# Decoder layer on one core: another PSUM bank for the x1 transposes, the denominators turned by a transpose, and the router's weight halves side by side in one matmul

## The reference

```
x  = layernorm(x + self(x))       # softmax(x x^T / 16), entries under 0.01 taken out, rest times x, plus a term of W
x  = layernorm(x + cross(x, ctx)) # 16 heads of 16: q, k, v with biases, masked softmax, @ Wo + bo
x  = layernorm(x + ffn(x))        # probs = softmax(x @ Wr) over 8 experts, top 2; sum of p_e * (x @ Wi[e]) @ Wo[e]
```

## Time and profile before

| | us |
|---|---|
| median of 3 runs (lowest, highest) | 889.59 (889.4, 890.37) |
| the profiled execution | 888.66 |
| its span, first to last instruction | 886.9 |
| TensorE busy (matmul) / loading weights | 846.5 / 737.9 |
| VectorE busy | 725.9 |
| ScalarE busy | 654.0 |
| GpSimd busy | 199.8 |
| mean granted TensorE clock | 0.993 of full |

### The profile page before, as it was taken

How to read it: one execution, slowest core, us unless ns; L and a number is a source line. 1 busy time by engine, 2 the same in 40 slices (tenths; PEclk the granted TensorE clock), 3 DMA queues, 4 the chain that set the end, 5 groups by cost and what they waited for, 6 DMA issues and landing times.

```text
span 886.9 us, 25688 instructions
## 1 busy us (share of the span) xinstructions
PE 846.5 (95%) x7972; PEld 737.9 (83%) x7972; DVE 725.9 (82%) x2772; ACT 654.0 (74%) x1961; POOL 199.8 (23%) x293
## 2 busy tenths in 40 slices
PE   4789999999999999999999999999999999999985
PEld 3678888888888888888888888888888988888874
DVE  3557888888888888888888888888888888888765
ACT  2468877777887777788777777877777787777760
POOL 2212222221222222222222222222222222222101
PEclk9899999999999999999999999999999999999998
DMA  8544444444334444433344443334444333433300
GB/s 257 159 120 98 106 104 106 105 120 98 93 99 101 103 107 120 99 91 99 98 110 106 117 103 93 99 98 107 105 116 115 85 99 95 107 79 85 85 12 11
DMA packets 89830, 91.09 MB, mean 103 GB/s; under 512 B 19440, under 2 KB 85600, under 8 KB 89696
## 3 DMA queue, kind: packets, MB, share of 16 engines
q1 hardware_dynamic: 89696, 89.45, 40.0%
HBM read 26.84 MB, written 3.67 MB: 34 GB/s over the span
## 4 chain that ended last, share of the span: by engine, by line
PE 89%; DVE 3%; SPq 3%; ACT 2%; issue 2%; DMA 1%; POOL 1%; POOLq 0%; DVEq 0%; ACTq 0%
PE psum L1024 22%; PE psum L908 18%; PE psum L899 10%; PE psum L924 10%; PE psum L974 7%; PE psum L967 7%; PE psum L956 3%; PE psum L988 3%; PE psum L945 1%; PE psum L981 1%; PE psum L938 1%; PE psum L950 1%; ACT x1T L483 1%; DMA wout_sb<-in_wout 1%; DVE mix L608 1%
## 5 line engine op out<-in xcount | busy, mean ns | idle before, releaser
L474 ACT ACTIVATE probs<-masked,nmax 112x375 f32<-112x375 f32 x512 | 312.4, 610 | 73.4 <-DVE nmax L594 72.7
L594 DVE CUSTOM_DVE_ANT_0 masked<-psum,mask_add 112x375 f32<-112x375 f32 x512 | 278.1, 544 | 70.8 <-PE psum L899 50.5
L504 ACT ACTIVATE probsT<-psum 125x336 f32<-125x336 f32 x512 | 227.6, 445 | 90.1 <-PE psum L908 89.7
L908 PE MATMUL psum<-const_sb,probs 112*125 112x112 f32 x1536 | 251.4, 272 | 0.1
L908 PEld LDWEIGHTS psum<-const_sb,probs 112*125 112x125 f32 x1536 | 236.8, 189 | 15.7 <-issue 6.6
L899 PE MATMUL psum<-k_stack,q_stack 96*112 96x376 f32 x512 | 203.7, 398 | 3.1 <-DMA k_stack<-k_hi 2.6
L417 POOL TENSOR_SCALAR var_eps<-moments 112x1 f32<-112x1 f32 x96 | 21.3, 222 | 500.2 <-DVE moments L698 210.2
L608 DVE SCALAR_TENSOR_TENSOR mix<-psum,gate,mix 112x256 f32<-112x256 f32 x224 | 108.1, 483 | 18.2 <-PE psum L1024 2.9
L1024 PE MATMUL psum<-we_hi,x_hi 128*112 128x512 f32 x256 | 110.9, 433 | 9.5 <-ACT x1T L483 7.7
L899 PEld LDWEIGHTS psum<-k_stack,q_stack 96*112 96x112 f32 x512 | 90.2, 176 | 21.1 <-issue 8.7
L1024 PE MATMUL psum<-we_hi,x_lo 128*112 128x512 f32 x256 | 101.5, 397 | 0.0
(11 more groups left out here) (110 smaller groups left out, 1477.5 us busy)
## 6 DMA issues: line engine op xcount, KB each, us to landing
k_stack<-k_hi SPq DMA_DIRECT2D x256, 93.8 KB, 2.2
q_stack<-q_hi SPq DMA_DIRECT2D x256, 56.0 KB, 2.0
ctx_sb<-in_context_T SPq DMA_DIRECT2D x32, 376.0 KB, 3.2
k_stack<-k_lo SPq DMA_DIRECT2D x128, 93.8 KB, 2.2
q_stack<-q_lo SPq DMA_DIRECT2D x128, 56.0 KB, 2.0
xT<-in_x_T SPq DMA_DIRECT2D x32, 112.0 KB, 2.2
x_sb<-in_x SPq DMA_DIRECT2D x32, 112.0 KB, 2.2
out_dram<-out_sb SPq DMA_DIRECT2D x32, 112.0 KB, 1.9
```

Source lines behind the costliest of these rows:

```text
L474: nc.scalar.activation(probs[:, n % RING, :], masked[:, n % RING, :], ACT.Exp, bias=nmax[:, n:n + 1], scale=-1.0, accum_out=probs_sum[a[1] ...
L504: nc.scalar.activation(probsT[:, i % TRING, :], psum[0:KP, T_BANKS[i % 2], 0:KT * TOK], ACT.Copy).then_inc(probsT_copied, 1)
L594: nc.vector.tensor_tensor_reduce(masked[:, n % RING, :], psum[0:TOK, S_BANKS[n % 2], 0:KEYS], mask_add[k][:, :], 1.0, 3.0e38, ALU.add, ALU ...
L908: mm = nc.tensor.transpose(psum[0:KP, T_BANKS[n % 2], j * TOK:(j + 1) * TOK], probs[:, n % RING, j * KP:(j + 1) * KP], ident[0:TOK, 0:TOK])
```

## The change

- x1T goes to bank G2 instead of G1. In G1 m0 is then preceded by m3 of the iteration before (its read ends with `e7`); in G2 x1T is preceded by V1, and qT by x1T.
- The two matmuls of rb become two transposes (`nc.tensor.transpose`) of the same `rden_wide`.
- `wr_hi` and `wr_lo` are replaced by one tile `wr_parts` with both halves, negated, side by side. Per chunk one matmul multiplies x2's high part with both (16 columns), a second adds low part times high half to columns 0 to 7: four matmuls instead of six. The logits come out negated.
- VectorE copies columns 8 to 15 to SBUF (`cross_logits`), waits for that, and then adds them to columns 0 to 7 and takes the minimum in one `tensor_tensor_reduce`, in place of the `tensor_reduce`. ScalarE's exponential reads the sum from SBUF with scale -1. The bank of lg is free once VectorE has read it, no longer only after the exponential.

```diff
-USES = [("x1T", 0, "G1"), ("m0", 1, "G1"), ...
+USES = [("x1T", 0, "G2"), ("m0", 1, "G1"), ...
-                 "lg": (act_steps, "gate_exp"), ...
+                 "lg": (dve_steps, "gate_max"), ...
-                            gate_exp[:, :], bank_of["lg"][0:TOK, 0:EXPERTS], ACT.Exp, bias=gate_nmax[:, :],
-                            scale=1.0, accum_out=gate_sum[:, :]).then_inc(act_join.did("gate_exp"), 1)
+                            gate_exp[:, :], neg_logits[:, :], ACT.Exp, bias=gate_nmax[:, :],
+                            scale=-1.0, accum_out=gate_sum[:, :]).then_inc(act_join.did("gate_exp"), 1)
-                            nc.vector.tensor_reduce(
-                                gate_nmax[:, :], bank_of["lg"][0:TOK, 0:EXPERTS], AX.X, ALU.max, negate=True)\
+                            nc.vector.tensor_copy(cross_logits[:, :], bank_of["lg"][0:TOK, EXPERTS:2 * EXPERTS])\
+                                .then_inc(dve_join.did("cross_logits"), 1)
+                            dve.wait_ge(dve_join.sem, dve_join.to("cross_logits", o))
+                            settle(dve)
+                            nc.vector.tensor_tensor_reduce(
+                                neg_logits[:, :], bank_of["lg"][0:TOK, 0:EXPERTS], cross_logits[:, :],
+                                1.0, 3.0e38, ALU.add, ALU.min, gate_nmax[:, :])\
                                   .then_inc(dve_join.did("gate_max"), 1)
-                    split_weights(((wr_sb, wr_hi, wr_lo),), 6)
+                    nc.vector.tensor_scalar(wr_parts[:, :, 0, :], wr_sb[:, :, :], -1.0, None, ALU.mult)\
+                      .then_inc(setup_dve, 1)
+                    ... (wr_parts[:, :, 1, :] = -wr_sb - wr_parts[:, :, 0, :])
-                            mm = nc.tensor.matmul(
+                            mm = nc.tensor.transpose(
                                 bank[:, c * TOK:(c + 1) * TOK],
                                 rden_wide[:, CHUNK_HEADS * c:CHUNK_HEADS * (c + 1), :].rearrange("q h d -> q (h d)"),
-                                ident[0:TOK, 0:TOK], start=True, stop=True)
+                                ident[0:TOK, 0:TOK])
                         if name == "lg":
                             pe.wait_ge(dve_join.sem, dve_join.to("x2_lo", o))
+                            for c in range(DC):
+                                nc.tensor.matmul(bank[0:TOK, 0:2 * EXPERTS], hi[:, c, :],
+                                                 wr_parts[:, c, :, :].rearrange("p h e -> p (h e)"),
+                                                 start=(c == 0), stop=False, skip_group_check=True)
+                                mm = nc.tensor.matmul(bank[0:TOK, 0:EXPERTS], lo[:, c, :], wr_parts[:, c, 0, :],
+                                                      start=False, stop=(c == DC - 1), skip_group_check=True)
```

More of the change, by code:

```diff
@@ L45 @@
 S_BANKS, T_BANKS, O_BANK, G_BANKS = (0, 1), (2, 3), 4, (5, 6, 7)
-USES = [("x1T", 0, "G1"), ("m0", 1, "G1"), ("rb", 1, "O"), ("qT", 2, "G2"), ("K0", 3, "G0"), ("Wo", 4, "G1"), ("Sc", 5, "G2"),
+USES = [("x1T", 0, "G2"), ("m0", 1, "G1"), ("rb", 1, "O"), ("qT", 2, "G2"), ("K0", 3, "G0"), ("Wo", 4, "G1"), ("Sc", 5, "G2"),
         ("K1", 6, "G1"), ("m1", 8, "G0"), ("V0", 9, "G2"), ("x2T", 10, "G1"), ("PT", 11, "G0"),
@@ L158, in decoder_layer @@
         wr_sb = sb("wr_sb", [128, DC, EXPERTS])
-        wr_hi = sb("wr_hi", [128, DC, EXPERTS], f32r)
-        wr_lo = sb("wr_lo", [128, DC, EXPERTS], f32r)
+        wr_parts = sb("wr_parts", [128, DC, 2, EXPERTS], f32r)
         wiT = sb("wiT", [128, EXPERTS_PER, DC, DIM])
@@ L228, in decoder_layer @@
         gate_sum = sb("gate_sum", [TOK, 1])
+        neg_logits = sb("neg_logits", [TOK, EXPERTS])
+        cross_logits = sb("cross_logits", [TOK, EXPERTS])
         gate_r = sb("gate_r", [TOK, 1])
@@ L272, in decoder_layer @@
             ("attn", ["rden", "rden_wide"]),
-            ("join", ["attnT", "y2", "stats2", "moments2", "x2", "x2_lo", "gate_max",
+            ("join", ["attnT", "y2", "stats2", "moments2", "x2", "x2_lo", "cross_logits", "gate_max",
                       "gate_r", "gate_p", "top_p", "top_i", "top_f", "gate_a", "gate_b", "gate"]),
@@ L289, in decoder_layer @@
                  "rb": (dve_steps, "attnT"), "Wo": (dve_steps, "y2"), "x2T": (dve_steps, "x2_lo"),
-                 "lg": (act_steps, "gate_exp"), "m0": (dve_steps, "e1"), "m1": (dve_steps, "e3"),
+                 "lg": (dve_steps, "gate_max"), "m0": (dve_steps, "e1"), "m1": (dve_steps, "e3"),
                  "m2": (dve_steps, "e5"), "m3": (dve_steps, "e7")}
@@ L868, in iteration @@
                 if it == -1:
-                    split_weights(((wr_sb, wr_hi, wr_lo),), 6)
+                    nc.vector.tensor_scalar(wr_parts[:, :, 0, :], wr_sb[:, :, :], -1.0, None, ALU.mult)\
+                      .then_inc(setup_dve, 1)
+                    dve.wait_ge(setup_dve, 7)
+                    nc.vector.scalar_tensor_tensor(
+                        out=wr_parts[:, :, 1, :], in0=wr_sb[:, :, :], scalar=-1.0,
+                        in1=wr_parts[:, :, 0, :].bitcast(fp32), op0=ALU.mult, op1=ALU.subtract)\
+                      .then_inc(setup_dve, 1)
             run(dve, iteration)
@@ L1011, in product @@
                             pe.wait_ge(dve_weights.sem, dve_weights.to(f"we_lo{EXPERTS_PER - 1}", o))
+                        hi, lo = (x2_hi[1 - k], x2_lo[1 - k]) if name == "lg" else (x2_hi[k], x2_lo[k])
                         if name == "lg":
                             pe.wait_ge(dve_join.sem, dve_join.to("x2_lo", o))
-                            hi, lo = x2_hi[1 - k], x2_lo[1 - k]
-                            w_hi, w_lo, width = wr_hi[:, :, :], wr_lo[:, :, :], EXPERTS
+                            for c in range(DC):
[4 more added lines that the diff above has]
+                                                      start=False, stop=(c == DC - 1), skip_group_check=True)
                         else:
-                            n, width, hi, lo = int(name[1]), 2 * DIM, x2_hi[k], x2_lo[k]
+                            n, width = int(name[1]), 2 * DIM
                             w_hi = we_hi[:, :, n * width:(n + 1) * width]
                             w_lo = we_lo[:, :, n * width:(n + 1) * width]
[L1021 to L1025, removed]
+                            parts = [(c, x_part, w_part) for c in range(DC)
+                                     for x_part, w_part in ((hi, w_hi), (hi, w_lo), (lo, w_hi))]
+                            for n, (c, x_part, w_part) in enumerate(parts):
+                                mm = nc.tensor.matmul(bank[0:TOK, 0:width], x_part[:, c, :], w_part[:, c, :],
+                                                      start=(n == 0), stop=(n == len(parts) - 1))
                     return mm
```

## The result

Median 867.54 us (865.43 to 869.25, 4 runs) against 889.5; ratio 0.9751, 95% interval 0.9731 to 0.9770. The profiled execution took 868.0 with a span of 866.2, so 20.7 of span are gone. The range was 863.8 to 881.0, the forecast 870.8.

The account below looks back on a forecast made before the run. TensorE, busy 25.51 of 25.79 us an iteration, sets the pace. It saves 0.82, waits 0.15 for y2 and keeps 0.67; 28 x 0.67 = 18.8 gives 870.8 us against the median, range 863.8 to 881.

Parts of the forecast that it names:

- x1T to G2: TensorE from scores to m0: the wait for ScalarE's copy of x1T goes, saving 0.48 us an iteration.
- rb by transposes: TensorE at rb: two transposes replace four instructions, 0.43 us becoming 0.19 in the chain, saving 0.24.
- lg: TensorE's router matmuls: two fewer save 0.20 us, of which at most 0.10 is left because V1 waits for e5.
- e5: VectorE's step of expert 5, done at 421.16; V1, loading at 421.30, must wait for it.
- The router step on VectorE: Copy and tensor_tensor_reduce take 0.25 us more; e6 absorbs a part, so 0.10 is the cost downstream.
- e6: VectorE's step of expert 6, behind the router step: starts about 0.10 us later, absorbing part of the 0.25.
- K1 waits for y2: TensorE's K1 weight load arrives 0.82 us early, waits 0.15 for VectorE's y2, and keeps 0.67 an iteration.
- S: Slack of a TensorE wait on VectorE; the smallest, at K1, was put at 0.67 us an iteration.
- The slack of 0.78 at head 2: Scores of head 4 load on TensorE and need VectorE's head 2; 0.78 us to spare, no new wait forecast.
- the first rival: TensorE keeps everything, 0.82 to 0.92 us in each of 28 iterations: 864 to 867 us; chance 0.27.
- TensorE's own sum: TensorE's saving an iteration before waits on VectorE: 0.48 + 0.24 + 0.10 = 0.82 us.
- the slower rival: TensorE's clock falls as matmuls give way to transposes, expert products slow down: +21.6 us, 911; chance 0.06.

Follow-up runs that it names:

- bank only: Kernel before with x1T in G2 and nothing else changed: 874.8 us, ratio 0.9836, iteration 25.28.
- the run with two copies: Changed kernel with the router's copy of 8 columns made three times, each waiting for the one ahead: 875.6 us, ratio 0.9830.
- e4's place: Changed kernel with VectorE's step of expert 4 moved ahead of head 14, nothing left out: 860.9 us, ratio 0.9676.
- router only: Kernel before with only the router's part: four matmuls, copy and tensor_tensor_reduce; 889.3 us, ratio 0.9999.

## Why the prediction was right, and the step that was wrong

- **x1T to G2: right.** 0.48 forecast, 0.52 measured. That is the iteration of bank only, and it is what the chain shows in the whole: from the x1T transposes to rb it takes 418.38 to 420.29, 1.91 us, and in the kernel before 426.97 to 429.40, 2.43:
```profile
426.97 0.36 PE psum L950 x2
```
The distance from scores to m0 alone, which the forecast was read from, fell by 0.44.
- **rb by transposes: right.** 0.24 forecast and measured; 0.43 became 0.20 in the chain.
- **lg: right in size and in its loss.** 0.098 from start to start holds for 16 columns, and V1's wait for e5 left 0.06 to 0.07 of the 0.20 where 0.10 was forecast. V1 loads at 412.69, 0.05 after e5 is done at 412.64.
- **The router step on VectorE: nearly right.** 0.25 forecast, 0.30 measured (0.53 less 0.23): copy to next step 0.34, not 0.23, with a hole of 0.18 that is labelled as the wait for the engine's own result; the `tensor_tensor_reduce` to moments1 is 0.19, where 0.25 was allowed. e6 absorbs most of it as forecast: counted from head 14, e6 starts 5.40 later, before 5.29, and head 1 8.33 later; from there the price is 0.1.
- **K1 waits for y2: wrong.** This step set S at 0.67, and it is what put the forecast 3.3 us too high. No such wait came; y2 is 14.16 behind head 14, before 14.73, so 0.57 earlier and not 0.25. I took the stretch from head 1 to head 5 as fixed, with 0.35 of idleness at its end. But attnT in it waited for TensorE's rb. In the kernel before, first TensorE, then VectorE:
```profile
403.46 0.59 PE L981 MATMUL psum<-const_sb,rden_wide 112*128 112x112 f32 x4
```
```profile
404.09 0.39 DVE L648 TENSOR_TENSOR attnT<-o_sb,psum 128x224 f32<-128x224 f32 x1
```
attnT starts 0.04 after rb ends (404.05). A hole that short has no label. With rb's end 0.8 earlier, attnT follows head 2 at once, and head 3 starts 10.51 behind head 14 instead of 10.64, although head 1 is 0.1 later; that is 0.23 of the missing 0.32. The iteration that the earlier trace rows shows is not typical here. A hole of 0.2 (before head 2, at 429.48) hid the wait for rb in it, so its attnT too followed head 2 at once; in the iterations without such a hole attnT starts 0.04 after rb, and head 3 stands at 10.62. The other 0.09 lies between q_hi and head 5. The labelled idleness counts from the end of q_hi, while in the changed kernel head 5 starts 0.09 before that end:
```profile
423.55 0.58 DVE L662 TENSOR_SCALAR q_hi<-q_sb,const_sb 128x224 fp32r<-128x224 f32 x2
424.04 0.54 DVE L595 CUSTOM_DVE_ANT_0 masked<-psum,mask_add 112x375 f32<-112x375 f32 x1
```
- **Head 1 left out.** It isn't among the waits that the prediction priced; the run with two copies shows that it, and not head 2 or K1, comes next. The slack of 0.78 at head 2 was read behind the hole at 429.48, too.
- **What came in the iteration was the first rival**, that TensorE keeps everything: 0.83 against 0.82 of TensorE's own sum (0.52 + 0.24 + 0.07 for 0.48 + 0.24 + 0.10). 28 x 0.83 is 23.2, yet the span fell by 20.7. Over the 27 distances read, 697.1 became 676.0: 21.1. 27 x 0.83 = 22.4; the long iterations take 1.3 of it (1.8 us over the median pace, before 0.5). The forecast's two errors, 0.16 too little an iteration and no long iterations, are of opposite sign. So that the time lies inside the forecast's own band, 867 to 876, is luck: with even iterations it would have been 867.5 - 1.3 = 866.2, below it.
- **The clock** stayed at 1.00 in the iteration, so the slower rival did not come about. The Trainium skill (TensorE: Matmul & The Clock Gate, Part 4: PE-mode transpose) says that transposes don't count as busy time in the same way. That made no difference that this trace shows, with a granted clock of 1.00 before and after.

## What to carry to other kernels

When one engine sets the pace, sum what it saves from start to start, and then price every wait of it on the others, in order, with the slack of each; a wait that is missing from the list (head 1 here) may be the first. Slack on the other engine is worth reading from its holes too, over more than one iteration. Some of its holes are waits for the pacing engine and vanish with the gain, even where they are too short to be labelled. A saving that is held at once by another engine's step can still be had by moving that step into a hole: here e4's place made a part worth nothing into 6 us.

## Not expected

- VectorE has a hole of 0.2 to 0.5 us at some six to nine places of a run, in steps that wait for nothing the profile shows. They come at the same steps in kernels with the same VectorE program: changed (337, 465, 490 us) and router only (344, 475, 501 us). Counted over all VectorE instructions that the trace records, those on semaphores included, each of these places has a number 128 n + 64: in the changed kernel the 832nd (209 us), 1472nd (337), 2112th (465), 2240th (490), 3008th (642), 3136th (667), 3392nd (718), 3520th (743) and 4032nd (857), in the kernel before among others the 704th (189) and 1728th (402). About a third of such numbers have a hole. What happens there was not settled. A hole cost nothing where VectorE had time to spare, and 0.15 to 0.4 where its result was due at once, in the kernel before too (161 and 189 us).
- A small VectorE copy of 8 columns that the next step waits for costs 0.19 when a copy follows and 0.34 when the step behind is the `tensor_tensor_reduce`, ahead of which the kernel has a semaphore step more (`settle`). Which of the two makes the difference was not tried.
